# Token shares of RWKV time mixing applied to the activations in place of the weights, and its steps placed anew beside a mixture of experts

## The reference

```python
x = ln0(x)                               # x4 in the kernel
h = ln1(x)
hp = time_shift(h)                       # the token before, zero for the first
k = (h * tmk + hp * (1 - tmk)) @ Wk.T    # key
v = (h * tmv + hp * (1 - tmv)) @ Wv.T    # value
r = (h * tmr + hp * (1 - tmr)) @ Wr.T    # receptance
x = x + (sigmoid(r) * wkv(decay, first, k, v)) @ Wo.T
c = ln2(x); cp = time_shift(c)
x = x + sigmoid((c * cmr + cp * (1 - cmr)) @ Wfr.T) * (relu((c * cmk + cp * (1 - cmk)) @ Wfk.T) ** 2 @ Wfv.T)
```

## Time and profile before

| | |
|---|---|
| runs | 497.91, 497.86, 498.1 us |
| the profiled execution | 496.6 us, its span 494.9 us |
| PE busy | 470.8 us (95%) |
| DVE busy | 389.5 us (79%) |
| POOL busy | 366.7 us (74%) |
| ACT busy | 355.9 us (72%) |
| PE's granted clock | 1.00 of full speed throughout |

### The profile page before, as it was taken

The page is one execution under the profiler, slowest core; times in us unless marked ns, Lnnn a source line. Parts: engine busy times, 40 slices in busy tenths (PEclk is TensorE's granted clock), DMA queues, the critical chain, the costliest instruction groups (busy, mean ns, idle before and its releaser), DMA issues.

```text
span 494.9 us, 10643 instructions
## 1 busy us (share of the span) xinstructions
PE 470.8 (95%) x3706; PEld 325.5 (66%) x3706; DVE 389.5 (79%) x1043; ACT 355.9 (72%) x687; POOL 366.7 (74%) x449
## 2 busy tenths in 40 slices
PE   7898999999899999999999999999999989999994
PEld 7575789988466666656566756576566766766663
DVE  5899999677767878799888897889887868487663
ACT  1699999774857767964996759695868576858551
POOL 4755896986485775899878978987989585366652
PEclk9999999999999999999999999999999999999999
DMA  8000212000200000000000000000000000000000
GB/s 270 20 2 11 66 53 66 1 1 3 71 1 1 1 1 2 3 0 1 2 1 1 3 1 1 1 1 2 2 23 1 1 1 23 2 2 1 21 1 23
DMA packets 7013, 8.51 MB, mean 17 GB/s; under 512 B 560, under 2 KB 5168, under 8 KB 6960
## 3 DMA queue, kind: packets, MB, share of 16 engines
q1 hardware_dynamic: 6960, 7.83, 4.9%
HBM read 6.78 MB, written 1.05 MB: 16 GB/s over the span
## 4 chain that ended last, share of the span: by engine, by line
PE 55%; DVE 9%; POOL 5%; ACT 3%; issue 2%; DVEq 0%; POOLq 0%; ACTq 0%
PE bank L1571 9%; PE bank L1575 9%; PE bank L1572 9%; PE bank L1590 5%; PE bank L1592 5%; PE bank L1591 5%; PE bank L1707 3%; PE bank L1690 2%; PE bank L1633 2%; DVE x L1941 2%; PE bank L1634 2%; POOL b_hc L2222 1%; PE bank L1597 1%; DVE b_hid L1925 1%; PE bank L1618 1%
## 5 line engine op out<-in xcount | busy, mean ns | idle before, releaser
L2160 POOL TENSOR_TENSOR b_hid_lo<-b_hid,b_hid_hi 128x512 f16<-128x512 f32 x144 | 168.0, 1179 | 51.4 <-ACT b_hid_hi L1769 49.3
L1925 DVE SCALAR_TENSOR_TENSOR b_hid<-bank,b_silu 128x512 f32<-128x512 f32 x144 | 97.7, 688 | 55.4 <-ACT b_silu L1762 38.1
L1762 ACT ACTIVATE b_silu<-bank 128x512 f32<-128x512 f32 x144 | 85.9, 597 | 57.6 <-PE bank L1575 56.5
L1571 PE MATMUL bank<-x_hi,wsplit 128*128 128x512 f16 x284 | 107.7, 379 | 2.4 <-ACT b_silu L1762 1.9
L1575 PE MATMUL bank<-x_lo,wsplit 128*128 128x512 f16 x284 | 107.6, 379 | 0.0
L1572 PE MATMUL bank<-x_hi,wsplit 128*128 128x512 f16 x284 | 107.6, 379 | 0.0
L1590 PE MATMUL bank<-wsplit,b_hid_hi 128*128 128x128 f16 x576 | 100.2, 219 | 4.3 <-DVE x L1941 2.6
L1769 ACT CAST b_hid_hi<-b_hid 128x512 f16<-128x512 f32 x144 | 88.2, 612 | 22.2 <-DVE b_hid L1925 22.0
L1592 PE MATMUL bank<-wsplit,b_hid_lo 128*128 128x128 f16 x576 | 100.2, 219 | 0.0
L1591 PE MATMUL bank<-wsplit,b_hid_hi 128*128 128x128 f16 x576 | 100.2, 219 | 0.0
L1941 DVE SCALAR_TENSOR_TENSOR x<-bank,b_w_branch,x 128x128 f32<-128x128 f32 x256 | 71.5, 342 | 15.5 <-PE bank L1592 15.4
(11 more groups left out here) (246 smaller groups left out, 946.4 us busy)
## 6 DMA issues: line engine op xcount, KB each, us to landing
moe_raw<-in_moe SPq DMA_DIRECT2D x9, 384.0 KB, 4.1
x<-in_x SPq DMA_DIRECT2D x4, 256.0 KB, 3.9
out<-x SPq DMA_DIRECT2D x4, 256.0 KB, 2.3
rope<-in_rope SPq DMA_DIRECT2D x1, 512.0 KB, 6.2
wzx<-in_wzx SPq DMA_DIRECT2D x1, 386.0 KB, 6.5
b_w_rkvo<-in_w_rkvo SPq DMA_DIRECT2D x1, 256.0 KB, 2.7
b_w_fk<-in_w_fk SPq DMA_DIRECT2D x1, 256.0 KB, 2.9
b_w_fv<-in_w_fv SPq DMA_DIRECT2D x1, 256.0 KB, 3.4
```

What stands on the lines that cost most here:

```text
L1571: nc.tensor.matmul(dst, hi, x_hi[:, q % 2, :], start=True, stop=False)
L1762: nc.scalar.activation(silu[:, 2 * (u % 2) + blk, :], gate_ps[blk][:, :], ACT.Silu, scale=GU_UNSCALE).then_inc(silu_ready, 1)
L1925: nc.vector.scalar_tensor_tensor(hid[:, 2 * (u % 2) + blk, :], up_ps[blk][:, :], GU_UNSCALE * H_SCALE, silu[:, 2 * (u % 2) + blk, :], ALU. ...
L2160: nc.gpsimd.tensor_tensor(hid_lo[:, slot, :], hid[:, 2 * (u % 2) + blk, :], hid_hi[:, slot, :], ALU.subtract).then_inc(lo_ready, 1)
```

## The change

The share of a token and of the token before it is applied to the activations and not to the weights. POOL makes step_h = hT - (hT one column earlier), once for a sequence (`step`). DVE makes shared_h[j] = step_h * share_j + (hT one column earlier), three tiles for a sequence (`share`), and `project` is one matmul with the weights as they are loaded. w_now, w_prev and `mixes` are gone. copy_h waits for the shares of the sequence before, since hT is one buffer. The semaphores shared_ready (three for a sequence, in the order key, receptance, value) and step_ready are new.

Most steps are given other places. Those of POOL and the shares stand in the diff; the others are (place before -> place after):

| engine | steps |
|---|---|
| PE | logits (0,1)->(0,0) of each slot; turn_h (16,1)->(15,0); key (16,2)->(16,0); output (24,0)->(22,0); hidden 0 to 2 (29,2)->(29,1); hidden 3 (30,0)->(29,1); gate_c (30,2)->(29,1); values (31,2) and (32,0)->(30,0); turn_x (8,0)->(7,2) of each slot |
| ACT | high_x (8,1)->(7,3) and apply_x (7,2),(7,3)->(2,1),(5,1), later (5,2), of each slot; normalise (13,2)->(12,3),(13,0); apply_h (15,2)->(14,2); copy_h (16,1)->(15,1); bounds (17,3)->(18,1); exponentials (18,3)->(18,2); copy_c (26,3)->(26,1); relus, squares 0 to 2 (29,3) to (30,1)->(29,1); relu 3, square 3 (31,0),(31,2)->(29,2); sigmoid (32,0)->(29,2); route_exp (0,3)->(0,2) of each slot; decay exponential unit 1->unit 5 |
| DVE | route_shift, route_first (0,2)->(0,0),(0,1), apply_x (7,0)->(5,1), ln_m1 statistics (6,1)->(4,1) of a slot; ln_a (12,1)->(11,0),(12,0); ln_b (15,0)->(14,0); scan_max (17,0)->(16,1); carry (17,1)->(17,0); negative_r (18,2)->(18,1); scan_num (20,1)->(20,0); divide (22,2),(23,0)->(20,2),(21,0); attend (23,1)->(21,1); join (24,0)->(22,0); ln_c (24,2),(25,0)->(23,1),(24,1); mix 0 (29,0)->(27,1); gated (32,2)->(30,1); ln_m2 (33,0)->(31,0),(31,1) |

```diff
-        w_now = sb("w_now", [P, 3, P])
-        w_prev = sb("w_prev", [P, 3, P])
...
+        step_h = sb("step_h", [P, SEQ])
+        shared_h = sb("shared_h", [P, 3, SEQ])
...
             def project(j, bank, made):
-                nc.tensor.matmul(bank[:, :], w_now[:, j, :], hT[:, 1:SEQ + 1], start=True, stop=False)
-                nc.tensor.matmul(bank[:, :], w_prev[:, j, :], hT[:, 0:SEQ], start=False, stop=True).then_inc(made, 1)
+                nc.tensor.matmul(bank[:, :], w_rkvo[:, j, :], shared_h[:, j, :], start=True, stop=True).then_inc(made, 1)
 
             def key(s):
                 if s == 0:
                     pe.wait_ge(routed, 2)
                     pe.wait_ge(zeroed, 1)
-                    pe.wait_ge(w_prev_ready, 3)
+                    pe.wait_ge(w_b_in, 16 * 4)
                 else:
                     pe.wait_ge(x4_ready, s)
-                pe.wait_ge(hT_ready, s + 1)
+                pe.wait_ge(shared_ready, 3 * s + 1)
                 project(0, ps_k, k_made)
 
             def value(s):
+                pe.wait_ge(shared_ready, 3 * s + 3)
                 pe.wait_ge(scores_read, s + 3)
                 project(1, ps_v, v_made)
 
             def receptance(s):
+                pe.wait_ge(shared_ready, 3 * s + 2)
                 pe.wait_ge(normT_ready, s + 2)
                 project(2, ps_t, r_made)
...
             def copy_h(s):
                 act.wait_ge(h_turned, s + 1)
+                if s:
+                    act.wait_ge(shared_ready, 3 * s)
                 nc.scalar.activation(hT[:, 1:SEQ + 1], ps_t[:, :], ACT.Identity,
                                      bias=col(core, "ln1_b"), scale=col(core, "ln1_w")).then_inc(hT_ready, 1)
...
+            def share(s, j):
+
+                made, which = ((k_made, 0), (r_made, 2), (v_made, 1))[j]
+                dve.wait_ge(step_ready, s + 1)
+                if s:
+                    dve.wait_ge(made, s)
+                nc.vector.scalar_tensor_tensor(shared_h[:, which, :], step_h[:], col(core, ("tmk", "tmv", "tmr")[which]),
+                                               hT[:, 0:SEQ], ALU.mult, ALU.add).then_inc(shared_ready, 1)
...
                         aggregate(ln_b, s, veps_b)
+                    if at == (15, 1):
+                        share(s, 0)
+                    if at == (16, 1):
+                        scan_max(s)
+                    if at == (16, 2):
+                        share(s, 1)
+                        share(s, 2)
                     if at == (17, 0):
-                        scan_max(s)
+                        carry(s)
                     if at == (17, 1):
-                        carry(s)
                         difference(s)
                         leads(s)
+                    if at == (18, 1):
+                        negative_r(s)
                     if at == (18, 2):
-                        negative_r(s)
                         scan_den(s)
...
-            def mixes():
-
-                pool.wait_ge(w_b_in, 16 * 4)
-                for j, name in enumerate(("tmk", "tmv", "tmr")):
-                    nc.gpsimd.tensor_scalar(w_now[:, j, :], w_rkvo[:, j, :], col(core, name), None,
-                                            ALU.mult).then_inc(w_now_ready, 1)
-                for j in range(3):
-                    pool.wait_ge(w_now_ready, j + 1)
-                    nc.gpsimd.tensor_tensor(w_prev[:, j, :], w_rkvo[:, j, :], w_now[:, j, :],
-                                            ALU.subtract).then_inc(w_prev_ready, 1)
+            def step(s):
+
+                if s == 0:
+                    pool.wait_ge(zeroed, 1)
+                else:
+                    pool.wait_ge(shared_ready, 3 * s)
+                pool.wait_ge(hT_ready, s + 1)
+                nc.gpsimd.tensor_tensor(step_h[:], hT[:, 1:SEQ + 1], hT[:, 0:SEQ], ALU.subtract).then_inc(step_ready, 1)
...
-                if (u, place) == (3, 0):
-                    mixes()
-                if (e, place) == (8, 0) and q + 1 < SLOTS:
+                if (e, place) == (7, 1) and q + 1 < SLOTS:
                     low_x(q + 1)
-                if (e, place) == (8, 0) and q < 2:
+                if (e, place) == (7, 2) and q < 2:
                     pool.wait_ge(veps_in, q + 1)
                     ln_rstd(nc, core, link, ln_m1, of_seq(q + 2), rstd_in)
                 for s in range(SEQS):
                     at = u - BRANCHES * s, place
-                    if at == (12, 0):
+                    if at == (11, 1):
                         pool.wait_ge(veps_a, s + 1)
                         ln_rstd(nc, core, link, ln_a, of_seq(s), rstd_a)
+                    if at == (12, 1):
+                        affine(s, 0)
+                    if at == (12, 2):
+                        affine(s, 1)
                     if at == (13, 1):
-                        affine(s, 0)
-                    if at == (13, 2):
-                        affine(s, 1)
-                    if at == (14, 2):
                         pool.wait_ge(veps_b, s + 1)
                         ln_rstd(nc, core, link, ln_b, of_seq(s), rstd_b)
-                    if at == (19, 0):
+                    if at == (14, 2):
+                        step(s)
+                    if at == (18, 1):
                         gate_r(s)
+                    if at == (18, 2):
                         first_values(s)
                     if at == (19, 1):
                         second_values(s)
-                    if at == (20, 0):
                         denominator(s, 0)
+                        denominator(s, 1)
+                        denominator(s, 2)
+                        numerator(s, 0)
                     if at == (20, 1):
-                        denominator(s, 1)
-                    if at == (20, 2):
-                        denominator(s, 2)
-                    if at == (21, 1):
-                        numerator(s, 0)
-                    if at == (22, 1):
                         numerator(s, 1)
-                    if at == (24, 2):
+                    if at == (24, 0):
                         pool.wait_ge(veps_c, s + 1)
                         ln_rstd(nc, core, link, ln_c, of_seq(s))
-                    if at == (25, 0):
                         apply_c(s, (0, 1))
+                    if at == (24, 2):
                         apply_c(s, (2, 3))
-                    if at == (27, 2):
+                    if at == (25, 2):
                         add_x4(s)
-                    if at == (28, 1):
                         difference(s)
-                    if at == (32, 1):
+                    if at == (30, 0):
                         add_rkv(s)
-                    if at == (32, 2):
+                    if at == (31, 1):
                         pool.wait_ge(veps_in, stats_before(s + SEQS))
                         ln_rstd(nc, core, link, ln_m2, of_seq(s), rstd_in)
 
```

More of the change, by code:

```diff
@@ L1714, in beside @@
                 q, e = divmod(u, BRANCHES)
-                if (e, place) == (0, 1) and q < SLOTS:
+                if (e, place) == (0, 0) and q < SLOTS:
                     logits(q)
@@ L1718, in beside @@
                     at = u - BRANCHES * s, place
-                    if at == (16, 1):
+                    if at == (15, 0):
                         turn_h(s)
-                    if at == (16, 2):
+                    if at == (16, 0):
                         key(s)
@@ L1725, in beside @@
                         value(s)
[L1726 removed]
+                    if at == (22, 0):
                         output(s)
@@ L1733, in beside @@
                         hidden(s, 2)
+                        hidden(s, 3)
+                        gate_c(s)
                     if at == (30, 0):
-                        hidden(s, 3)
-                    if at == (30, 2):
-                        gate_c(s)
-                    if at == (31, 2):
                         values(s, (0, 1))
-                    if at == (32, 0):
                         values(s, (2, 3))
-                if (e, place) == (8, 0) and q + 1 < SLOTS:
+                if (e, place) == (7, 2) and q + 1 < SLOTS:
                     turn_x(q + 1)
@@ L2080, in beside @@
                 q, e = divmod(u, BRANCHES)
-                if (e, place) == (0, 2):
+                if (e, place) == (0, 0):
                     route_shift(q)
-                if (e, place) == (0, 2):
+                if (e, place) == (0, 1):
                     route_first(q)
@@ L2088, in beside @@
                     route_weigh(q)
-                if (e, place) == (7, 0) and SEQS <= q + 1 < SLOTS:
+                if (e, place) == (5, 1) and SEQS <= q + 1 < SLOTS:
                     apply_x(q + 1, (0, 1))
-                if (e, place) == (6, 1) and q < 2:
+                if (e, place) == (4, 1) and q < 2:
                     stats(ln_m1, x, q + 2)
-                if (e, place) == (6, 2) and q < 2:
-                    aggregate(ln_m1, q + 2, veps_in)
+                if (u, place) == (4, 2):
```

(8 more changed lines are left out.)

63 lines of the change are left out of this document (31 added, 32 removed).

## The result

The changed kernel takes 495.49 us (median of 20 runs, 494.47 to 497.46) beside 497.28 us for the kernel before (20 runs, 495.71 to 498.18): a ratio of 0.9967, 95% interval 0.9957 to 0.9977. It is faster, by 1.6 us by the ratio and 1.8 by the medians; 4.7 were forecast. The direction held, the size did not. The time before that the forecast started from, 497.91 us, is the median of three of those 20 runs and lies 0.6 above the median of all. The profiled execution is 494.47 us with a span of 492.7.

A forecast was written before the change was run, and what follows sets the result against it. PE was taken as the bound, with POOL and DVE at 86 to 91% where sequences overlap. The stretch terms summed to -4.7 us, giving 493.2 us, range 489.5 to 496.9.

The forecast's parts named there:

- Part 1, the matmuls: On PE, `project` runs one matmul in place of two: 12 matmuls go, 10.3 us less PE work.
- Part 2, the shares: POOL gets four steps of 1.04 us; DVE gets 12 shares, three adding 2.2 to 5.1 us per stretch, taken as 4.
- rival B: Slower: DVE and POOL become the bound as shares and POOL operations block each other; 500.5 us, chance 0.18.
- Part 4, the row of five: Five POOL products in a row in unit 19 delay low(19,1) to +21.2 us; PE waits 4.2 us before down(19).
- The term of units 9 to 17: PE work falls 0.86 us, but hn is ready 0.8 us after PE asks: -0.1 us.
- Units 18 to 26: POOL's busy time plus forced idle time, less spill, gives 47.5 us where it was 46.19: +1.3 us.
- Units 27 to 53: Three stretches: -1.4, -1.2 and -2.7 us, the last with the 1.3 us wait for b_hc at unit 53 gone.
- Units 0 and 1: route_exp ahead of the first cast and the decay exponential gone: ACT returns to silu sooner, -0.6 us.
- The end: The rest of the kernel and the 2.6 us wait at the very end stay unchanged: 0.

The follow-up runs named there:

- r2_pool_light: The changed kernel with POOL's seven products of the recurrence on 128 of 512 tokens: 494.49 us, 0.9949 of the kernel before.
- p1: The changed kernel's places with the earlier arithmetic (two matmuls per product, no step, no shares): 498.94 us, 1.0045 of the kernel before.
- p2: The changed kernel with every key, receptance and value product computed twice into the same bank: 499.81 us, 1.0056 of the kernel before.
- p4: The changed kernel with turn_h, copy_h, step, share 0, key and scan_max each one place later: 509.79 us, 1.0255 of the kernel before.
- p3: The changed kernel with each share computed for 128 of the 512 tokens: 494.22 us, 0.9946 of the kernel before.
- q2: The changed kernel with POOL's row of five products broken once, two steps moved behind subtractions: 496.50 us, 0.9990 of the kernel before.
- r1: The split row of q2 in the changed kernel, with DVE's divides one place later, attend, output and join also moved: 499.37 us, 1.0042 of the kernel before.
- s4: The changed kernel with DVE's ln_m1 statistics for sequence 3 in unit 15 in place of unit 13: 496.40 us, 0.9988 of the kernel before.
- s1: The changed kernel with the routing steps of slots 1 to 7 at the places of the kernel before: 503.06 us, 1.0113 of the kernel before.
- t1: s1 with PE's value product behind down, (18,2) in place of (18,1): 495.06 us, 0.9965 of the kernel before.
- r3: The changed kernel with DVE's two scans on 128 of 512 tokens and reciprocals on 64 of 256: 493.86 us, 0.9939 of the kernel before.
- q3: The changed kernel with the recurrence's second half, denominator to b_hc, at the places of the kernel before: 506.34 us, 1.0183 of the kernel before.
- r4: The changed kernel with ACT's copy of the value tile at (19,1) in place of (18,3): 497.80 us, 1.0020 of the kernel before.

## Why the prediction was half right

The direction held. The size did not, because two terms of the sum were wrong in their mechanism. In units 9 to 17 the chain to hn was walked to 0.8 us late and was 1.9, and the wait of unit 11 stood at nothing: +1.58 us in place of -0.1. In units 18 to 26 the time was taken to be POOL's busy time plus its forced idle time; the stretch took +2.77 in place of +1.3, and r2_pool_light shows that POOL's load alone doesn't set it: 6.7 us of POOL's work less shorten it by 1.23. DVE's chain ends within 1.2 us of POOL's there.

- **Part 1, the matmuls.** 24 records fewer were right, and 10.3 us of PE's work (10.0 measured). It isn't the time gained, which the sum allowed for by its floors: p1 and p2 put the worth at 3.9 and 4.3 us.
- **Part 2, the shares.** Mis-sized: 4 us for three was taken from the upper end (1.70 each), they measured 0.75 in the median, and DVE's busy time in units 27 to 35 rose by 1.96 us and not by 4. POOL's rose by 2.30 in place of 1.04. That shares take 1.7 where POOL is busy came true for one of twelve, the first, which started behind a POOL operation (1.63). Where a share started first, POOL's operation was the one that took longer. The rows of the changed kernel around the start of unit 25, DVE then POOL, show who paid:

```profile
237.59 0.75 DVE L2021 SCALAR_TENSOR_TENSOR b_shared_h<-b_step_h,cols,b_hT 128x512 f32<-128x512 f32 x1
...
242.62 1.59 DVE L2021 SCALAR_TENSOR_TENSOR b_shared_h<-b_step_h,cols,b_hT 128x512 f32<-128x512 f32 x2
```

```profile
237.66 1.55 POOL L1421 TENSOR_TENSOR ln_cm_rstd<-ln_cm_veps,mhalf 128x4 f32<-128x4 f32 x1
...
242.98 1.82 POOL L2239 TENSOR_SCALAR b_hc<-b_x,ln_cm_rstd,ln_cm_nbias 128x128 f32<-128x128 f32 x2
```

The share that starts first takes its 0.75; POOL's operation beside it takes 1.55 in place of 1.01, two b_hc tiles 1.82 in place of 0.89 (the undisturbed figures are in p4's rows above). That fits the lock of the Trainium skill's page "SBUF — State Buffer", section "SBUF: two separate sides": the later one waits. The rival B built on it did not come about: three quarters of the shares' work are worth 1.0 to 1.4 us (p3).
- **Part 4, the row of five.** A wait of 4.2 us was forecast before down(19). Measured, PE waits 2.53 us for b_hid_lo there. Ahead of it, in units 19, 20 and 21, stand waits of 0.26, 1.37 and 0.97, the last two for DVE, which the walk didn't have; with them it is 5.1 in all. low(19,1) ends 22.1 us after the start of unit 18, not 21.2. POOL in the changed kernel, beside the earlier trace rows:

```profile
206.80 1.50 POOL L2209 TENSOR_SCALAR b_e_r<-b_e_r 128x512 f32<-128x512 f32 x1 [2.49 <-ACT b_e_r L1824]
...
214.30 2.06 POOL L2223 TENSOR_TENSOR b_den<-b_den,b_expo 128x512 f32<-128x512 f32 x1
216.44 1.27 POOL L2226 TENSOR_TENSOR b_den_r<-b_den,b_e_r 128x512 f32<-128x512 f32 x1
217.67 1.27 POOL L2231 TENSOR_TENSOR b_num<-b_expo,b_aa 128x512 f32<-128x512 f32 x1
219.02 2.26 POOL L2179 TENSOR_TENSOR b_hid_lo<-b_hid,b_hid_hi 128x512 f16<-128x512 f32 x2
```

The product at 214.30 took 2.06 and not the 1.27 of the earlier trace rows, beside DVE's scan; the earlier trace rows had shown that price (1.27 to 2.19), and the sum left it out here. The place was right, and that the sum of the waits came out near 4.2 was partly luck, since nearly half of it hangs on DVE. That the row causes it was too simple: in q2, r1 and r2 DVE's divide and its addition end within 0.1 to 1.5 us of it, so taking the row away leaves much of the wait.
- **The term of units 9 to 17** failed, by 1.7 us, half of the whole miss. hn was walked to 0.8 us late and is 1.9 late. s4 shows 0.9 us of this wait to be DVE's ln_m1 statistics, moved to unit 13 ahead of the addition and of the ln_b statistics; the working priced "the ln_m1 step" on POOL and had no line for it on DVE. A further 0.42 is the wait of unit 11 for DVE's addition, which the routing places cause (gone in s1 and t1), priced at nothing. The arithmetic was to give 0.86 in this stretch; p1 shows 0.58.
- **Units 18 to 26** missed by 1.5. In the sum's own terms POOL's busy time is 44.46 for 43.7 and its idle time 4.5 for 3.8. But r2 and r3 show that neither POOL's nor DVE's load alone sets this time, so the miss can't be split by these terms. The waits of units 24 and 25 (1.1 and 0.6) weren't in the walk.
- **Units 27 to 53** came to -5.5 for -5.3. Right in sum, partly by luck: DVE's share price was too high, which made up for the waits of units 28 and 29 (0.17 and 0.37) and for b_hn in units 33 and 42 (1.96 each), which had no line of their own. The 1.3 us for b_hc at unit 53 did go.
- **Units 0 and 1** (-0.45 for -0.6): near in sum. The wait for b_silu fell by 1.2 and not 0.6, and a wait for b_hid of 0.5 came. The end, priced at 0, costs 0.38, again DVE's addition behind the routing, in unit 65.

The measured terms add up to -1.3 from unit 0 on, and the timed runs say -1.6 to -1.8. What stays open is which order of DVE and POOL would free units 18 to 26. Six kernels moved steps there (q2, q3, r1, r4, s1, t1), and none shortened that stretch by more than 0.33 us. Whether the two loads together set it isn't shown either, since they weren't lightened in one kernel.

## What to carry to other kernels

When three engines are each at 85 to 95% in a stretch, work taken off one of them can be worth much less than its length: here 10.3 us of matmuls were worth about 4, and in units 18 to 26 2.58 us were worth 0.24. Price a moved step in every queue that it enters, the small statistics too, and take a product's contended duration where the traces show the two side by side. The places of two steps in in-order queues were worth 11 us here, because another sequence's steps stood ahead of one of them. And before two profiles are compared stretch by stretch, look at the granted clock in both: here it alone made 0.5 to 1.1 us.

## What the runs showed of the hardware

PE's granted clock fell from 2.4 to 1.2 GHz for 3.4 us at a time, behind a wait or in it, in some executions and not in others of the same kernel. In the profiled execution of the changed kernel taken last (t2_changed_again), PE waited 2.5 us in unit 21, until 222.6 us, and this is the clock ahead of, in and behind the next 3.5 us:

```profile
199.30:222.90 23.60, 19.12 (x160) 11.46 (x158) 20.95 (x52) 16.30 (x30) 20.70 (x19) 1.00 0.00 1
222.90:226.40 3.50, 3.50 (x26) 2.43 (x24) 3.43 (x13) 1.31 (x3) 3.03 (x5) 0.53 0.00 0
226.40:248.80 22.40, 21.25 (x180) 13.71 (x179) 18.99 (x52) 15.61 (x32) 20.75 (x24) 1.00 0.01 2
```

Units 18 to 26 took 49.46 us there and 48.96 in the profile above, which has the same wait and a clock of 1.00 in all the stretches shown: 0.5 us. In t1, r1 and r4 such a piece in unit 42, behind a wait of 2.1 us for b_hn, made units 36 to 44 1.04 to 1.08 us longer than units 27 to 35, which are otherwise alike. In p4_turn_h_later, with three waits of about 4 us before the key, the clock fell at each. A wait of PE can so cost more than its length. What decides whether it falls is not shown: the wait of unit 21 is equally long in both executions of the changed kernel.
